# Causal attention beside a quantized FFN on eight cores: double-buffered weight rounding, and the second half of P·V moved to other PSUM banks

## The chip, the cores and the metric

The kernel runs on the 8 NeuronCores of one Trainium2 chip. All cores run the same program, each on its own rows, with no exchange between them. The metric is the device time of the slowest core in microseconds. Engines are named as in the profile: PE (TensorE), DVE (VectorE), ACT (ScalarE), POOL (GpSimd), SP (SyncE, which here only issues DMAs).

## What is computed

```python
xn = _layernorm(x, axis=-1)                       # x: (4, 4096, 2048) float32
K = xn @ Wk.T;  Q = xn @ Wq.T;  V = xn @ Wv.T     # all weights 2048 x 2048
probs = softmax(where(causal, Q @ K.T / sqrt(2048), -inf))
att = round(probs @ V * 10000) / 10000
xq = fake_quant(xn, 8, -1)        # scale per row
kq = fake_quant(kernel, 8, 0)     # scale per column of the FFN weight
bq = fake_quant(bias, 8, -1)
y = fake_quant(relu(xq @ kq + bq), 8, -1)
out = x + att + y
# fake_quant: s = max|x| / 127, round(x / s) clipped to +-127, times s
```

Two cores share a batch. Each makes K and V of the whole sequence and the output of every second block of 256 rows, 2048 rows in 16 tiles of 128.

## The kernel before, in words

`build_nc` writes the program as five stages with a barrier after each. Every instruction is recorded by `Prog.step` (a compute instruction) or `Prog.dma` with the `Buf` objects that it reads and writes. From these the waits are made: an instruction waits for the last writer of what it reads, and for the last writer and all readers since then of what it writes. This holds for instructions of its own engine too: PE then waits for sPE, the semaphore that its own earlier matmul raises when it is done. A `Buf` is a name and not a range of addresses, so one `Buf` for two PSUM banks makes a writer of the second wait for the writer of the first. Each engine issues in the order in which its steps were recorded, and so does each queue; nothing is reordered.

Stage 1 (L390 to L484): layernorm of all rows, V and K into HBM (`vS`, `kS`), PE L451 and L471. Stage 2 (to L640): layernorm and rounding of the core's own rows, Q into HBM (`qS`), PE L627.

Stage 3 quantizes the FFN weight, `fker`, 2048 x 2048, in 16 tiles of 128 rows (1 MB each). It has two passes over it, with two slots `fk` for the loads.

- The abs-max pass: SP loads a tile (L697), ACT takes the absolute value into `tab` (L699), DVE takes the running maximum over the tiles (L702 for the first, L704). There is one `tab`.
- A preamble: the maxima are transposed (L707), turned into reciprocals (L727), spread over all partitions (L737, L740), and the bias is quantized (L746 to L779).
- The rounding pass: POOL multiplies the tile by the reciprocal scales into `tab` (L786), ACT converts it into integers `ci3` (L788), DVE takes the remainder f3 from `tab` and `ci3` (L790), adds a correction (L793, reads f3 and `ci3`, writes r13) and scales (L796, writes the bf16 weight). There is one `tab`, one `ci3`, one `f3` and one `r13`. POOL's next multiply waits for L790, the last reader of `tab`.

Stage 4 is the FFN itself: 16 tiles, PE L845 with four PSUM banks a tile.

Stage 5 is attention, in 8 groups g of two query tiles (T = 0, 1). Group g looks at 512(g+1) keys:

- SP loads the Q tiles of the next group (`load_qt`, L943, 32 small DMAs), then x and the FFN result (L957, L959), then K in strips of 512 keys into two slots (`load_ktb`, L965, 16 DMAs a strip). The first strip of the next group is loaded ahead.
- QK: for each strip and each T, 16 matmuls into one bank of `psA` (L981); ACT or DVE copies the scores out (L991, L986), DVE takes the maximum (L995).
- First half of P·V: for each strip exp (L1021), transposes of P through the two banks `psTh` (L364), and 4 key chunks kc of 128. For each kc SP loads 128 x 1024 of V into one of two slots `vt` (L1030), and PE does 2 matmuls of 512 columns for each T (L1037). They sum up in `psB`, T = 0 in the first two banks, T = 1 in the other two, with one `Buf` each, bB[0] and bB[1].
- Second half of P·V, the other 1024 columns of V: nkc = 4(g+1) chunks, loads L1055, matmuls L1073. Here T = 0 sums up in `psA` (two banks, bA[0] and bA[1]) and T = 1 in `psN` (two banks, bT[0] and bT[1], the ones of the transposes).
- Behind each half, for each T, the evacuation: ACT L1093 reads the sums and writes the integers `ci4`, DVE L1096 reads the sums and `ci4`, L1099 reads `ci4` again, L1103 adds to the output tile. There is one `ci4`, so ACT's L1093 of T = 1 waits for DVE's L1099 of T = 0. PE's order is: first half, second half, QK of the next group.

A "step" is one kc of the second or first half: four matmuls, T = 0 twice, T = 1 twice. PSUM has 8 banks of 512 float32 columns: `psA` is 0 and 1, `psB` 2 to 5, `psN` and `psTh` 6 and 7.

## Time and profile before

| | us |
|---|---|
| median of 2 runs (5878.27 to 5885.0) | 5881.63 |
| the profiled execution's own time | 5880.86 |
| its span, on the slowest core (core 4) | 5879.3 |
| spans of the eight cores | 5795.6 to 5879.3 |
| PE busy | 3634.8 (62%) |
| DVE busy | 1085.1 (18%) |
| ACT busy | 678.6 (12%) |
| POOL busy | 208.2 (4%) |

The span runs from the first to the last instruction of one core; the time of an execution also has what lies around it, 1.6 us here. Busy time is that of an engine over the whole span, so it mixes the five stages. The granted clock is the share of TensorE's full speed that it was given: 1.00 is 2.4 GHz and 0.50 is 1.2 GHz. L12 is line 12 of the kernel before.

### The profile page before, as it was taken

What the parts mean: (1) busy time and instruction counts of PE and PEld (TensorE: products, weight loads), DVE (VectorE), ACT (ScalarE), POOL (GpSimd) and SP (SyncE); (2) the same over time, 40 slices, a digit from 0 to 9 for tenths busy, and PEclk for the clock granted to TensorE, in tenths of its full rate; (3) what the DMA queues carried; (4) which work ended last, traced back from release to release, by engine and by line L of the source; (5) the groups of instructions that cost most, each with busy time, mean ns of one, the idle gap of its engine ahead of it and who ended that gap; (6) DMA issues with size and microseconds to landing.
All of it is one profiled execution on the core that took longest, in us unless ns stands there. A gap on an engine that the chain in (4) does not pass through costs nothing.

```text
span 5879.3 us, 41336 instructions; the slowest of 8 cores (5795.6 to 5879.3 us)
## 1 busy us (share of the span) xinstructions
PE 3634.8 (62%) x9801; PEld 982.1 (17%) x9801; DVE 1085.1 (18%) x1473; ACT 678.6 (12%) x861; POOL 208.2 (4%) x87
## 2 busy tenths in 40 slices
PE   2787787787784375757821386144564747566776
PEld 0222222222221111111100022000111111111111
DVE  1110110010011403030037655011101011101001
ACT  1110110110101303021021121000000000000000
POOL 1000000000000000000003300010000000000000
PEclk9989999989987555555555598555555555555556
DMA  8110110110004101000032111132233232232422
GB/s 158 51 50 16 51 50 22 45 50 24 36 21 87 59 21 49 16 29 23 12 117 79 54 55 44 56 101 92 78 105 104 80 106 83 81 109 82 136 64 99
DMA packets 288082, 380.87 MB, mean 65 GB/s; under 512 B 123617, under 2 KB 222081, under 8 KB 273537
## 3 DMA queue, kind: packets, MB, share of 16 engines
q1 hardware_dynamic: 210866, 277.50, 14.8%
q10 hardware_dynamic: 69888, 75.51, 3.5%
q0 software_dynamic: 7120, 25.22, 2.6%
q8 instruction: 114, 1.87, 0.1%
q14 instruction: 94, 0.77, 0.0%
HBM read 327.83 MB, written 75.51 MB: 69 GB/s over the span
## 4 chain that ended last, share of the span: by engine, by line
PE 55%; DMA 15%; issue 14%; DVE 7%; ACT 4%; SPq 2%; POOL 2%; another core or an unknown queue 1%; DVEq 0%; ACTq 0%; POOLq 0%
PE pspool L471 13%; PE pspool L981 10%; DMA pool<-qS 8%; PE pspool L627 8%; PE pspool L451 8%; DMA pool<-vS 5%; PE pspool L845 5%; PE pspool L1037 4%; PE pspool L1073 2%; PE pspool L428 2%; POOL pool L786 2%; SPq L965 1%; PE pspool L364 1%; PE pspool L597 1%; PE pspool L581 1%
## 5 line engine op out<-in xcount | busy, mean ns | idle before, releaser
L981 PE MATMUL pspool<-pool 128*128 128x512 bf16 x1152 | 663.1, 586 | 652.3 <-DMA pool<-kS 475.4
L471 PE MATMUL pspool<-pool 128*128 128x512 bf16 x2048 | 751.9, 377 | 286.3 <-PE pspool L471 1.8
L627 PE MATMUL pspool<-pool 128*128 128x512 bf16 x1024 | 589.1, 587 | 272.2 <-ACT pool L631 128.7
L451 PE MATMUL pspool<-pool 128*128 128x512 bf16 x2048 | 492.7, 404 | 86.3 <-DMA pool<-wvT 41.3
L845 PE MATMUL pspool<-pool 128*128 128x512 bf16 x1024 | 276.7, 394 | 220.6 <-DMA pool<-nxS 182.4
L1037 PE MATMUL pspool<-pool 128*128 128x512 bf16 x576 | 299.9, 590 | 81.3 <-DMA pool<-vS 37.8
L471 PEld LDWEIGHTS pspool<-pool 128*128 128x128 bf16 x2048 | 196.0, 96 | 842.4 <-issue 837.9
L981 PEld LDWEIGHTS pspool<-pool 128*128 128x128 bf16 x1152 | 121.5, 105 | 1195.7 <-issue 1192.7
L1073 PE MATMUL pspool<-pool 128*128 128x512 bf16 x576 | 228.0, 544 | 113.6 <-DMA pool<-vS 111.5
L451 PEld LDWEIGHTS pspool<-pool 128*128 128x128 bf16 x2048 | 209.5, 102 | 366.1 <-issue 161.8
L627 PEld LDWEIGHTS pspool<-pool 128*128 128x128 bf16 x1024 | 107.2, 106 | 752.3 <-issue 751.0
L431 DVE COPY pool<-pspool 128x512 bf16<-128x512 bf16 x128 | 54.4, 425 | 954.1 <-PE pspool L428 954.1
L995 DVE TENSOR_REDUCE pool<-pool 128x1 f32<-128x512 f32 x72 | 49.4, 686 | 825.6 <-ACT pool L991 823.9
L475 ACT ACTIVATE pool<-pspool 128x512 bf16<-128x512 f32 x128 | 76.4, 597 | 991.0 <-PE pspool L471 938.2
L428 PE MATMUL pspool<-pool 128*128 128x128 bf16 x512 | 116.3, 259 | 119.9 <-DVE pool L351 62.5
L334 ACT ACTIVATE pool<-pool 128x2048 bf16<-128x2048 f32 x48 | 91.5, 1906 | 606.5 <-PE pspool L451 469.6
L1008 POOL TENSOR_TENSOR pool<-pool 128x2048 f32<-128x2048 f32 x16 | 78.4, 4919 | 2297.9 <-DVE pool L1005 2297.9
L845 PEld LDWEIGHTS pspool<-pool 128*128 128x128 bf16 x1024 | 83.5, 98 | 414.9 <-issue 355.1
L364 PE MATMUL pspool<-pool 128*128 128x128 bf16 x288 | 76.7, 266 | 116.2 <-ACT pool L1021 84.0
L991 ACT ACTIVATE pool<-pspool 128x512 f32<-128x512 f32 x56 | 33.4, 597 | 861.3 <-PE pspool L981 861.3
L581 PE MATMUL pspool<-pool 128*128 128x128 bf16 x256 | 61.9, 265 | 111.3 <-DVE pool L351 44.3
L584 DVE COPY pool<-pspool 128x512 bf16<-128x512 bf16 x64 | 27.2, 424 | 525.9 <-PE pspool L581 514.1
(118 smaller groups left out, 1951.5 us busy)
## 6 DMA issues: line engine op xcount, KB each, us to landing
pool<-kS SPq DMA_DIRECT2D x576, 128.0 KB, 3.0
pool<-vS SPq DMA_DIRECT2D x288, 256.0 KB, 2.7
pool<-emb SPq DMA_DIRECT2D x32, 1024.0 KB, 4.8
pool<-x_own SPq DMA_DIRECT2D x32, 1024.0 KB, 5.0
pool<-fker SPq DMA_DIRECT2D x32, 1024.0 KB, 5.0
vS<-pool ACTq DMA_DIRECT2D x32, 512.0 KB, 2.6
kS<-pool ACTq DMA_DIRECT2D x128, 128.0 KB, 1.9
out<-pool ACTq DMA_DIRECT2D x16, 1024.0 KB, 4.6
```

Of the source, the lines that this page charges most:

```text
L334: p.step("ACT", lambda e: e.activation(sq_ap, xap, AF.Copy, accum_out=s1), reads=[b_x], writes=[b_sq, btg])
L364: p.step("PE", lambda e, o=psl, i=sap: e.transpose(o, i, identb), reads=[b_src, b_identb], writes=[bT[half]])
L428: p.step("PE", lambda e, o=psl, i=sap: e.transpose(o, i, identb), reads=[b_xnb4[t], b_identb], writes=[bT[half]])
L451: e.matmul(pv, xnT[:, 512 * c + 128 * t:512 * c + 128 * t + 128], W2[:, E * c + fo:E * c + fo + fw], start=st, stop=sp),
L471: e.matmul(pk, W1[:, E * ce + 128 * ca:E * ce + 128 * ca + 128], xnT[:, 512 * ce:512 * ce + 512], start=st, stop=sp),
L581: p.step("PE", lambda e, o=psl, i=sap: e.transpose(o, i, identb), reads=[b_xnb24[t], b_identb], writes=[bT[half]])
L627: e.matmul(pk, WQ[:, E * ce + 128 * ca:E * ce + 128 * ca + 128], xnT2[:, 512 * ce:512 * ce + 512], start=st, stop=sp),
L786: p.step("POOL", lambda e, sl=sl: e.tensor_mul(tab, fk[sl], rcb), reads=[b_fk[sl], b_rcb], writes=[b_tab])
L845: st=(c == 0), sp=(c == NCH - 1): e.matmul(pv, nxt[sl][:, 128 * c:128 * c + 128], NK[:, E * c + fo:E * c + fo + fw], start=st, stop=sp),
L981: st=(c == 0), sp=(c == NCH - 1): e.matmul(pa, qt[par][T][:, 128 * c:128 * c + 128], ktb[ks][:, 512 * c:512 * (c + 1)], start=st, stop=sp),
L1037: st=(kc == 0), sp=(kc == nkc - 1): e.matmul(pv, PT[T][:, 128 * kc:128 * kc + 128], vt[vs_][:, fo:fo + fw], start=st, stop=sp),
L1073: st=(kc == 0), sp=(kc == nkc - 1): e.matmul(pv, PT[T][:, 128 * kc:128 * kc + 128], vt[vs_][:, fo:fo + fw], start=st, stop=sp),
```

## The change

In stage 3 `tab` and `ci3` get a second buffer each, `tabB` and `ci3B`, and tile c uses buffer c % 2, in both passes. `f3` and `r13` stay single (`fs3` and `b_fs3` list the same buffer twice).

In stage 5 the matmuls of the second half of P·V write `psB`, T = 0 its first two banks and T = 1 the other two, with bB[T] as their `Buf`; the evacuation reads both halves from there. `psA` is then written by QK only and the banks of `psN` by the transposes only.

```diff
+        o_tabB = al.take(E)
+        o_ci3B = al.take(E)
...
+        tabs = [tab, cf(o_tabB, E)]
+        cis = [ci3, cI(o_ci3B, E)]
+        fs3 = [f3, f3]
...
+        b_tabs = [b_tab, Buf("tabB")]
...
+        b_cis = [b_ci3, Buf("ci3B")]
+        b_fs3 = [b_f3, b_f3]
...
-            p.step("ACT", lambda e, sl=sl: e.activation(tab, fk[sl], AF.Abs),
-                   reads=[b_fk[sl]], writes=[b_tab])
+            p.step("ACT", lambda e, sl=sl: e.activation(tabs[sl], fk[sl], AF.Abs),
+                   reads=[b_fk[sl]], writes=[b_tabs[sl]])
...
-                p.step("DVE", lambda e: e.tensor_max(Mt, Mt, tab), reads=[b_tab, b_M], writes=[b_M])
+                p.step("DVE", lambda e, sl=sl: e.tensor_max(Mt, Mt, tabs[sl]),
+                       reads=[b_tabs[sl], b_M], writes=[b_M])
...
-            p.step("POOL", lambda e, sl=sl: e.tensor_mul(tab, fk[sl], rcb),
-                   reads=[b_fk[sl], b_rcb], writes=[b_tab])
-            p.step("ACT", lambda e: e.activation(ci3, tab, AF.Copy, bias=128.0),
-                   reads=[b_tab], writes=[b_ci3])
-            p.step("DVE", lambda e: e.scalar_tensor_tensor(
-                f3, tab, 128.0, ci3, op0=ALU.add, op1=ALU.subtract),
-                reads=[b_tab, b_ci3], writes=[b_f3])
+            p.step("POOL", lambda e, sl=sl: e.tensor_mul(tabs[sl], fk[sl], rcb),
+                   reads=[b_fk[sl], b_rcb], writes=[b_tabs[sl]])
+            p.step("ACT", lambda e, sl=sl: e.activation(cis[sl], tabs[sl], AF.Copy, bias=128.0),
+                   reads=[b_tabs[sl]], writes=[b_cis[sl]])
+            p.step("DVE", lambda e, sl=sl: e.scalar_tensor_tensor(
+                fs3[sl], tabs[sl], 128.0, cis[sl], op0=ALU.add, op1=ALU.subtract),
+                reads=[b_tabs[sl], b_cis[sl]], writes=[b_fs3[sl]])
...
-                                if T == 0 and PVW <= 512:
...
-                                elif T == 0:
-                                    pv = psA[:, fo:fo + fw]
-                                    wb_ = bA[fo // 512]
-                                else:
-                                    pv = psN[:, fo:fo + fw]
-                                    wb_ = bT[fo // 512]
+                                pv = psB[:, PVW * T + fo:PVW * T + fo + fw]
...
-                                    reads=[b_PT[T][kc // 4], b_vt[vs_]], writes=[wb_])
+                                    reads=[b_PT[T][kc // 4], b_vt[vs_]], writes=[bB[T]])
...
-                    if sweep == 0:
-                        pvh = psB[:, PVW * T:PVW * T + EH]
-                        rdb = [bB[T]]
...
+                    pvh = psB[:, PVW * T:PVW * T + EH]
+                    rdb = [bB[T]]
```

No instruction moves to another place; their waits change. PE before, in the first attention group, from the last step of the first half of P·V (L1037) to the second (L1073). z_vt0 and z_vt1 are the landings of V in its two slots, sPE, sAC and sDV the progress of PE, ACT and DVE:

```order
L1037 MATMUL pspool<-pool 128x512 [waits z_vt1]
L1037 MATMUL pspool<-pool 128x512 [waits sPE]
L1037 MATMUL pspool<-pool 128x512
L1037 MATMUL pspool<-pool 128x512 [waits sPE]
L1073 MATMUL pspool<-pool 128x512 [waits z_vt0]
L1073 MATMUL pspool<-pool 128x512 x3
L1073 MATMUL pspool<-pool 128x512 [waits z_vt1,sPE]
L1073 MATMUL pspool<-pool 128x512 [waits sPE] x3
```

The three matmuls behind the first of L1073 wait for nothing. The sPE of the later ones is for the matmul of the step before in the same bank. The same place in the changed kernel, where the lines are L1047 and L1072:

```order
L1047 MATMUL pspool<-pool 128x512 [waits z_vt1]
L1047 MATMUL pspool<-pool 128x512 [waits sPE]
L1047 MATMUL pspool<-pool 128x512
L1047 MATMUL pspool<-pool 128x512 [waits sPE]
L1072 MATMUL pspool<-pool 128x512 [waits z_vt0,sAC,sDV]
L1072 MATMUL pspool<-pool 128x512 [waits sPE]
L1072 MATMUL pspool<-pool 128x512 [waits sAC,sDV]
L1072 MATMUL pspool<-pool 128x512 [waits sPE]
L1072 MATMUL pspool<-pool 128x512 [waits z_vt1]
L1072 MATMUL pspool<-pool 128x512 [waits sPE]
L1072 MATMUL pspool<-pool 128x512
L1072 MATMUL pspool<-pool 128x512 [waits sPE]
```

The first matmul of each T now waits for ACT and DVE, and in each step the second and the fourth wait for the one ahead of them, as in L1047.

POOL before, at the start of the rounding pass (z_fk0 and z_fk1 are the landings of the weight tile, sPL POOL's own progress):

```order
L718 DMA pool<-rowS 1x16x128 [waits z_rowW]
L786 TENSOR_TENSOR pool<-pool 128x2048 [waits z_fk0,sDV,sAC]
L786 TENSOR_TENSOR pool<-pool 128x2048 [waits z_fk1,sPL,sAC,sDV]
L786 TENSOR_TENSOR pool<-pool 128x2048 [waits z_fk0,sPL,sAC,sDV]
L786 TENSOR_TENSOR pool<-pool 128x2048 [waits z_fk1,sPL,sAC,sDV]
```

And in the changed kernel, where the multiply is L796:

```order
L728 DMA pool<-rowS 1x16x128 [waits z_rowW]
L796 TENSOR_TENSOR pool<-pool 128x2048 [waits z_fk0,sDV,sAC]
L796 TENSOR_TENSOR pool<-pool 128x2048 [waits z_fk1,sAC]
L796 TENSOR_TENSOR pool<-pool 128x2048 [waits z_fk0,sPL,sAC,sDV]
L796 TENSOR_TENSOR pool<-pool 128x2048 [waits z_fk1,sPL,sAC,sDV]
```

The second multiply has lost its wait for DVE; from the third on each waits for the DVE instruction two tiles back.

## Rows read from the trace of the kernel before

**Rows 1.** Stages: length, busy us (x) of PE, PEld, DVE, ACT, POOL, PEclk, DMA, GB/s.

```profile
1850.00:2971.00 1121.00, 708.04 (x1536) 160.63 (x1536) 199.67 (x368) 209.88 (x257) 8.45 (x16) 0.50 0.14 38
2971.00:3321.00 350.00, 32.03 (x41) 8.96 (x41) 247.78 (x107) 65.21 (x35) 102.44 (x18) 0.50 0.29 99
3321.00:3640.00 319.00, 276.67 (x1024) 83.45 (x1024) 172.72 (x173) 61.72 (x45) 0.00 (x0) 0.94 0.17 48
3640.00:5880.00 2240.00, 1261.02 (x2592) 271.46 (x2592) 256.47 (x404) 130.01 (x236) 78.42 (x16) 0.53 0.28 91
```

**Rows 2.** Abs-max pass: timeline (start, length, what), L697's landing, one stretch.

```profile
2978.31 1.91 ACT L699 ACTIVATE pool<-pool 128x2048 f32<-128x2048 f32 x1 [7.82 <-DMA pool<-fker]
...
2986.10 1.91 ACT L699 ACTIVATE pool<-pool 128x2048 f32<-128x2048 f32 x1 [2.56 <-DVE pool L704]
...
2990.57 1.91 ACT L699 ACTIVATE pool<-pool 128x2048 f32<-128x2048 f32 x1 [2.56 <-DVE pool L704]
...
3046.25 2.29 DVE L704 TENSOR_TENSOR pool<-pool 128x2048 f32<-128x2048 f32 x1 [2.17 <-ACT pool L699]
...
DMA to landing us min/median/max: 4.7/4.8/7.9
...
2990.00:3000.00 10.00, 0.00 (x0) 0.00 (x0) 5.06 (x3) 4.31 (x3) 0.00 (x0) 0.50 0.72 255
```

**Rows 3.** The rounding pass: one row of the waits (us, times, longest), then the timeline.

```profile
POOL pool L786 <- DVE pool L790: 102.1, 15, 34.1
...
3103.38 4.49 POOL L786 TENSOR_TENSOR pool<-pool 128x2048 f32<-128x2048 f32 x1 [33.71 <-DVE pool L740]
...
3289.05 6.60 POOL L786 TENSOR_TENSOR pool<-pool 128x2048 f32<-128x2048 f32 x1 [4.71 <-DVE pool L790]
3291.41 6.39 DVE L796 SCALAR_TENSOR_TENSOR pool<-pool 128x2048 bf16<-128x2048 f32 x1
...
3300.36 6.61 POOL L786 TENSOR_TENSOR pool<-pool 128x2048 f32<-128x2048 f32 x1 [4.71 <-DVE pool L790]
...
3314.03 2.29 DVE L796 SCALAR_TENSOR_TENSOR pool<-pool 128x2048 bf16<-128x2048 f32 x1
```

**Rows 4.** Timeline of attention's first group, around the step between P·V's halves.

```profile
3828.24 0.58 PE L1037 MATMUL pspool<-pool 128*128 128x512 bf16 x1 [1.98 <-DMA pool<-vS]
3828.98 1.01 PE L1037 MATMUL pspool<-pool 128*128 128x512 bf16 x2
3830.14 2.17 PE L1037 MATMUL pspool<-pool 128*128 128x512 bf16 x4
...
3833.47 4.89 PE L1037 MATMUL pspool<-pool 128*128 128x512 bf16 x8 [0.43 <-DMA pool<-vS]
...
3838.88 1.86 PE L1073 MATMUL pspool<-pool 128*128 128x512 bf16 x4 [0.52 <-DMA pool<-vS]
...
3842.52 1.28 DVE L1096 SCALAR_TENSOR_TENSOR pool<-pspool,pool 128x1024 f32<-128x1024 f32 x1
3843.57 1.60 PE L1073 MATMUL pspool<-pool 128*128 128x512 bf16 x4 [0.31 <-DMA pool<-vS]
...
3846.36 1.02 PE L1073 MATMUL pspool<-pool 128*128 128x512 bf16 x4 [1.19 <-DMA pool<-vS]
```

**Rows 5.** Timeline of SP's queue and of PE at the turn of groups; waits.

```profile
3836.04 7.63 SPq L1055 DMA_DIRECT2D pool<-vS  x4
3843.76 65.69 SPq L943 DMA_DIRECT2D pool<-qS  x32
...
5786.47 70.50 SPq L1055 DMA_DIRECT2D pool<-vS  x32
...
3926.26 0.58 PE L981 MATMUL pspool<-pool 128*128 128x512 bf16 x1 [53.38 <-DMA pool<-kS]
...
PE pspool L981 <- DVE pool L1096: 15.5, 7, 2.5
```

**Rows 6.** Groups by line: L1037 and L1073 (busy us, mean ns | idle before).

```profile
L1037 PE MATMUL pspool<-pool 128*128 128x512 bf16 x576 | 299.9, 590 | 81.3 <-DMA pool<-vS 37.8
L1073 PE MATMUL pspool<-pool 128*128 128x512 bf16 x576 | 228.0, 544 | 113.6 <-DMA pool<-vS 111.5
```

More of the change, by code:

```diff
@@ L698, in build_nc @@
                 out=fk[sl], in_=fker[128 * c:128 * (c + 1), :]), writes=[b_fk[sl]])
-            p.step("ACT", lambda e, sl=sl: e.activation(tab, fk[sl], AF.Abs),
-                   reads=[b_fk[sl]], writes=[b_tab])
+            p.step("ACT", lambda e, sl=sl: e.activation(tabs[sl], fk[sl], AF.Abs),
+                   reads=[b_fk[sl]], writes=[b_tabs[sl]])
             if c == 0:
-                p.step("DVE", lambda e: e.tensor_copy(Mt, tab), reads=[b_tab], writes=[b_M])
-            else:
-                p.step("DVE", lambda e: e.tensor_max(Mt, Mt, tab), reads=[b_tab, b_M], writes=[b_M])
+                p.step("DVE", lambda e, sl=sl: e.tensor_copy(Mt, tabs[sl]),
+                       reads=[b_tabs[sl]], writes=[b_M])
+            else:
+                p.step("DVE", lambda e, sl=sl: e.tensor_max(Mt, Mt, tabs[sl]),
+                       reads=[b_tabs[sl], b_M], writes=[b_M])
         for t in range(NCH):
@@ L785, in build_nc @@
                 reads=[b_fk[sl]], writes=[b_fk[sl]])
-            p.step("POOL", lambda e, sl=sl: e.tensor_mul(tab, fk[sl], rcb),
-                   reads=[b_fk[sl], b_rcb], writes=[b_tab])
-            p.step("ACT", lambda e: e.activation(ci3, tab, AF.Copy, bias=128.0),
-                   reads=[b_tab], writes=[b_ci3])
-            p.step("DVE", lambda e: e.scalar_tensor_tensor(
-                f3, tab, 128.0, ci3, op0=ALU.add, op1=ALU.subtract),
-                reads=[b_tab, b_ci3], writes=[b_f3])
-            p.step("DVE", lambda e: e.scalar_tensor_tensor(
-                r13, f3, 0.5, ci3, op0=ALU.is_gt, op1=ALU.add),
-                reads=[b_f3, b_ci3], writes=[b_r13])
+            p.step("POOL", lambda e, sl=sl: e.tensor_mul(tabs[sl], fk[sl], rcb),
[5 more added lines that the diff above has]
+                reads=[b_tabs[sl], b_cis[sl]], writes=[b_fs3[sl]])
+            p.step("DVE", lambda e, sl=sl: e.scalar_tensor_tensor(
+                r13, fs3[sl], 0.5, cis[sl], op0=ALU.is_gt, op1=ALU.add),
+                reads=[b_fs3[sl], b_cis[sl]], writes=[b_r13])
             p.step("DVE", lambda e, c=c: e.scalar_tensor_tensor(
@@ L1059, in build_nc @@
                             for (fo, fw) in _splits(EH):
-                                if T == 0 and PVW <= 512:
-                                    pv = psA[:, fo:fo + fw]
-                                    wb_ = bA[0]
-                                elif T == 1 and PVW <= 512:
-                                    pv = psA[:, 512 + fo:512 + fo + fw]
-                                    wb_ = bA[1]
-                                elif T == 0:
-                                    pv = psA[:, fo:fo + fw]
-                                    wb_ = bA[fo // 512]
-                                else:
-                                    pv = psN[:, fo:fo + fw]
-                                    wb_ = bT[fo // 512]
+                                pv = psB[:, PVW * T + fo:PVW * T + fo + fw]
                                 p.step("PE", lambda e, pv=pv, T=T, kc=kc, vs_=vs_, fo=fo, fw=fw,
@@ L1080, in build_nc @@
                     rsc = tiny(sg, 2)
-                    if sweep == 0:
-                        pvh = psB[:, PVW * T:PVW * T + EH]
-                        rdb = [bB[T]]
-                    elif PVW <= 512:
-                        pvh = psA[:, 512 * T:512 * T + EH]
-                        rdb = [bA[T]]
-                    elif T == 0:
-                        pvh = psA[:, 0:EH]
-                        rdb = [bA[0], bA[1]]
-                    else:
-                        pvh = psN[:, 0:EH]
-                        rdb = [bT[0], bT[1]]
+                    pvh = psB[:, PVW * T:PVW * T + EH]
+                    rdb = [bB[T]]
                     p.step("ACT", lambda e, pvh=pvh, rsc=rsc: e.activation(
```

## The prediction

> **What bounds the kernel now.** I first read the busy times by stage [rows 1]. Barriers separate the stages, so each stage has its own limit and a gain in one passes whole into the start of the next. The change touches two of them: the quantization of the FFN weight (2971 to 3321 us) and attention (3640 to 5880 us). In the first the reader sees TensorE nearly empty, 32 us of 350, and VectorE busy for 248. In the second TensorE is busy for 1261 of 2240 us with a granted clock of 0.53, so it runs at its lower level, 1.2 GHz, for most of it.
>
> Then the timelines. The abs-max pass is a chain of two engines [rows 2]: an ACT Abs of 1.91 us, VectorE's max of 2.29, and an ACT that sat idle 2.56 us for VectorE because both share one buffer, `tab`. The pitch is 2990.57 − 2986.10 = 4.47 us. The rounding pass has a pitch of 3300.36 − 3289.05 = 11.31 us, and the table of waits says that GpSimd waits for L790 in it, 102.1 us in 15 times [rows 3]. In attention I read the step from the first half of P·V (L1037) to the second (L1073) [rows 4], the queue of SP [rows 5] and the means of the two matmul groups [rows 6].
>
> **Rounding pass: two buffers for `tab` and `ci3`.** Taken alone the wait of 102.1 us promises a pitch near the longer engine. The durations speak against it [rows 3]. The same GpSimd multiply takes 4.49 us where no wide VectorE instruction runs and 6.61 us where one does; L796 takes 6.39 us beside it and 2.29 us without. 2.29 + 4.1 = 6.4: the later one waits until the other is done and then runs at its own speed. So they run by turns, and a turn of the loop costs 4.49 + 3 × 2.29 = 11.36 us. The pitch is 11.31. The loop is already full, and another buffer adds no time in which both could run. What it does bring: the second multiply need not wait for L790 any more and runs at about 3108 us, in VectorE's preamble, where the first one [rows 3] ran at its full speed beside small copies out of PSUM. After that GpSimd is one tile ahead and the cadence is the same, until the last round has no multiply beside it. That takes one stay of 4.1 to 4.5 us out of the chain: **−4.3 us**. Bounds: 0 and −62 (the second is a rival below).
> The Trainium skill (SBUF — State Buffer, section Who interferes with whom) says the same of the cause: VectorE and GpSimd share one port pair, a VectorE instruction with two SBUF inputs contends with a GpSimd instruction that reads SBUF, and the loser blocks fully. The trace agrees, 6.39 against 2.29 us. By this rule the pass gains only the one multiply; with ports that don't interfere it would gain the 62 us.
>
> **Abs-max pass.** With two `tab` the ACT waits for a load instead. A load takes 4.8 us from issue to landing in the median, 4.7 to 7.9 [rows 2], and is issued when the Abs of its slot is done. Two slots give a pitch of (1.91 + 0.1 + 4.8 + 0.1)/2 = 3.5 us; VectorE alone would need 2.4. But the DMA engines are at 0.72 now, with 255 GB/s [rows 2]; at 4.47/3.5 times the rate that would be 0.92, so loads will stretch. I take 5.3 us for a load, pitch 3.7. From the first Abs to the end of the last max there are 3048.54 − 2978.31 = 70.2 us now; 14 rounds at 0.77 less give **−11 us**. Bounds: 0 (the DMA gives no more than now) and −20 (a pitch of 3.0, the 1.05 MB of a tile at 255/0.72 = 354 GB/s).
>
> **P·V, second half, in psB.** Three things change.
> 1. *A wait for the evacuation.* The first matmul of T=1 now needs L1096 of T=1 in the first half to be done, and that comes behind L1093, L1096 and L1099 of T=0, since `ci4` is single: it ends at 3842.52 + 1.28 = 3843.80 [rows 4]. TensorE issues in order, so all of the second half stands behind it. Before, this matmul pair began 0.86 us behind 3838.88, at 3839.74; now at 3843.87. That is 4.1 us, 4.4 at the end of this k step. The next step's load has long landed, so it follows at once, also 4.3 late. 8 groups × 4.3 = +34 us. Bounds per group: 3.3 and 4.6.
> 2. *A wait of each second matmul for its neighbour.* Before, four buffers stood for the four banks of L1073; now bB[T] stands for two banks, and the order of instructions shows a wait for sPE on each second matmul, as in L1037. The trace prices it. Four L1073 in a step take 1.86 us: starts 0.43 apart and 0.58 for the last. In L1037 the second starts 0.74 behind the first (3828.24 to 3828.98), the third 0.43 later, the fourth 0.73 after that [rows 4]. So a step takes 0.74 + 0.43 + 0.73 + 0.58 = 2.48 us. Now what sets the pitch: V has two slots, a slot is loaded again when its step is done, and some 3 us pass from there to the start of the step after the next (3838.88 + 1.86 = 3840.74 to 3843.57 is 2.83). Two steps take one step and one load, in L1037 5.23 and 5.41 us (starts at 3828.24, 3833.47, 3838.88). That is 2.66 a step. Now: the eight runs of V loads in the second half on SP, the first and the last of which stand in [rows 5], have 144 loads over 136 pitches and sum to 324.2 us: 2.38 a step. Past the first two steps of each group 144 − 16 = 128 steps remain, at 0.28 to 0.30 more: +37 us. Bounds: 0.16 and 0.40 a step, 20 and 51 us.
> 3. *psA and psN stay free.* The next group's first QK matmul no longer waits for L1096: 15.5 us in 7 times now. That counts only where nothing later is waited for. In the first six groups TensorE stops again after 32 matmuls, for K, for 53.38 us in the row [rows 5]. These K loads stand on SP behind 32 loads of Q, which take 65.69 us and start when the last V load is out. So there the gain is swallowed, and what delays the V loads passes whole. Only before the last group is no Q loaded, and there 15.5/7 = 2.2 us are won: **−2 us**.
> Together +34 + 37 − 2 = **+69 us** for attention.
>
> **Sum.** 5880.86 us is the profiled execution's own time, 1.6 above its span and within 1 us of the median of the runs. 5880.9 − 4.3 − 11 + 69 = 5934.6, so **5935 us**, 0.9% more.
>
> **The rivals.**
> *A, only the stall counts.* If the wait between banks were hidden, as the load sets the pitch, the steps would keep 2.38: 5880.9 − 15.3 + 8 × 3.5 − 2 = 5892. For it: L1073 waits for V 111.5 us in 117 times, so there is slack. Against: the slot is freed when the step is done, so a longer step pushes the load too, and L1037 shows 2.66 with the same waits.
> *B, the loop does overlap.* A pitch of 3 × 2.29 + 0.3 = 7.2 us instead of 11.31 takes 15 × 4.1 = 62 us off, 58 more than counted: 5877, not slower than before. For it: the wait table. Against: the durations. It decides if GpSimd can slip in without stretching L790 to L796.
> *C, the clock.* L1073 reaches 2.4 GHz in stretches, as in the four matmuls in 1.02 us at 3846.36 [rows 4]; mean 544 ns against 590 in L1037 [rows 6]. If the denser second half ran at 2.4 GHz throughout, a step would take 0.52 + 0.22 + 0.52 + 0.37 = 1.63 us (0.22 apart and 0.37 long in that row, and the 0.15 us of a wait that L1037 shows twice a step), the pitch (1.63 + 2.9)/2 = 2.27: −14 instead of +37, 5884 in all. Against: L1037, with the very waits, stays near 1.2.
> *D, slower by far.* The FFN stage that follows begins 15 us earlier. It ran at 0.94 of the clock [rows 1], while the Q projection just before the quantization stayed at 0.50 for 1121 us. If the clock does not rise, its 1024 matmuls take 0.43 us each, 437 us and not the 319 of the stage now: +118, 6053. It decides once TensorE stays at 1.2 GHz through the stage's first 50 us and beyond. Against: its matmuls have no waits between neighbours, and the start differs in nothing but its moment.
>
> **How the numbers follow.** Forecast 0.66 (its own range 5908 to 5962), A 0.13, B 0.06, C 0.07, D 0.03; 0.05 for mixtures beyond. The range of 5888 to 5966 takes in A and the forecast, most of the bounds of the terms. A measurement of this kernel tells about 2% from no change: 5764 to 5999. Faster by more than that needs B and C and more, 0.01; slower needs D or all terms at their upper ends, 0.05; within, 0.94.
>
> **What would show each step.** Right: Abs pitch near 3.7; loop pitch still 11.3 with 6.4 and 6.6 us pairs and an early second multiply; SP's runs of V loads in the second half 2.6 to 2.7 a load (the last group's 31 pitches over 82 us, not 70.50); the wait for K still near 53 us. Wrong: a loop pitch near 7, L1073's starts 0.43 apart for all four, a wait for V that vanishes, or a clock other than 0.5 to 0.55 in attention.

## The result, and the profile after

| | before | after |
|---|---|---|
| median, us (runs) | 5881.21 (14) | 5946.75 (15) |
| lowest, us | 5864.72 | 5938.50 |
| ratio, 95% interval | | 1.0094 [1.0068, 1.0120] |
| profiled execution: own time, slowest span | 5880.86, 5879.3 (core 4) | 6005.56, 6003.6 (core 2) |

The changed kernel is 0.9% slower. Ratios leave out executions in which a whole die was longer at a lower granted clock (up to 6355.99 us after the change). In the profiled execution of the changed kernel cores 2 and 3 reached stage 3 at 3030 and 3018 us, the other six at 2963 to 2972 like those of before, with nothing changed up to there, so its own time lies 59 us above the median. Therefore core 4 is compared in both, and lengths of stages are given as means over the eight cores.

| mean over 8 cores, us | before | after |
|---|---|---|
| stage 3, first Abs to first FFN matmul | 343.1 | 329.5 |
| from there to the first QK matmul | 461.3 | 468.0 |
| attention, first QK matmul to the end | 2061.5 | 2145.0 |
| of it SP's eight runs of V loads, second half | 319.5 | 404.0 |

Stage 3 gave 13.6 us and attention took 83.5, which is what the second half of P·V took: its runs of V loads are 84.5 us longer.

The stages on core 4 (columns as in [rows 1]):

```profile
1850.00:2966.00 1116.00, 708.22 (x1536) 159.83 (x1536) 199.72 (x368) 209.71 (x256) 5.12 (x10) 0.50 0.14 38
2966.00:3298.00 332.00, 32.01 (x41) 8.97 (x41) 242.42 (x107) 65.11 (x35) 100.28 (x18) 0.50 0.30 104
3298.00:3607.00 309.00, 269.29 (x1024) 83.08 (x1024) 170.29 (x171) 61.72 (x45) 0.00 (x0) 0.97 0.17 49
3607.00:5928.00 2321.00, 1337.99 (x2592) 253.44 (x2592) 258.93 (x406) 130.09 (x236) 78.13 (x16) 0.51 0.27 88
```

Against [rows 1] PE is busy for 77 us more in attention with the same 2592 matmuls, and its granted clock went from 0.53 to 0.51. FFN kept its high clock. The abs-max pass on core 4, the same view as [rows 2] (Abs is L707, max L713):

```profile
2972.19 1.91 ACT L707 ACTIVATE pool<-pool 128x2048 f32<-128x2048 f32 x1 [7.61 <-DMA pool<-fker]
...
2998.28 1.91 ACT L707 ACTIVATE pool<-pool 128x2048 f32<-128x2048 f32 x1 [1.97 <-DMA pool<-fker]
3001.98 1.91 ACT L707 ACTIVATE pool<-pool 128x2048 f32<-128x2048 f32 x1 [1.78 <-DMA pool<-fker]
...
3030.40 2.29 DVE L713 TENSOR_TENSOR pool<-pool 128x2048 f32<-128x2048 f32 x1 [1.87 <-ACT pool L707]
```

One stretch of the same pass (columns as in the stages):

```profile
2990.00:3000.00 10.00, 0.00 (x0) 0.00 (x0) 5.99 (x3) 5.54 (x3) 0.00 (x0) 0.50 0.79 271
```

From issue to landing a load (L705) now takes:

```profile
DMA to landing us min/median/max: 4.7/5.3/7.8
```

The Abs now waits for its load and no longer for VectorE. The pass takes 3032.69 − 2972.19 = 60.5 us and not 70.2. The load takes 5.3 us in the median, as the prediction had put in, and not 4.8. The DMA share rose from 0.72 to 0.79 only, and not to the 0.92 that the prediction gave as the reason. The rounding pass, as [rows 3] (multiply L796, f3 L800, scaling L806), first the wait, then the timeline:

```profile
POOL pool L796 <- DVE pool L800: 90.5, 14, 29.6
```

```profile
3087.50 8.96 POOL L796 TENSOR_TENSOR pool<-pool 128x2048 f32<-128x2048 f32 x2 [33.71 <-DVE pool L750]
...
3259.54 6.60 POOL L796 TENSOR_TENSOR pool<-pool 128x2048 f32<-128x2048 f32 x1 [4.50 <-DVE pool L800]
3261.90 6.40 DVE L806 SCALAR_TENSOR_TENSOR pool<-pool 128x2048 bf16<-128x2048 f32 x1
...
3270.64 6.60 POOL L796 TENSOR_TENSOR pool<-pool 128x2048 f32<-128x2048 f32 x1 [4.50 <-DVE pool L800]
...
3291.09 2.29 DVE L806 SCALAR_TENSOR_TENSOR pool<-pool 128x2048 bf16<-128x2048 f32 x1
```

The first two multiplies run in one stretch of 8.96 us, 4.48 each; after that the pairs of 6.60 and 6.40 us return. The pitch is 3270.64 − 3259.54 = 11.10 us.

The step between the halves of P·V in the first group, as [rows 4] (L1072 is the second half, L1085 the evacuation's DVE instruction):

```profile
3808.59 1.32 PE L1072 MATMUL pspool<-pool 128*128 128x512 bf16 x2 [1.64 <-DVE pool L1085]
3811.10 1.28 DVE L1085 SCALAR_TENSOR_TENSOR pool<-pspool,pool 128x1024 f32<-128x1024 f32 x1
3812.53 3.64 PE L1072 MATMUL pspool<-pool 128*128 128x512 bf16 x6 [2.62 <-DVE pool L1085]
3816.98 2.48 PE L1072 MATMUL pspool<-pool 128*128 128x512 bf16 x4 [0.81 <-DMA pool<-vS]
3819.89 2.48 PE L1072 MATMUL pspool<-pool 128*128 128x512 bf16 x4 [0.43 <-DMA pool<-vS]
```

T=0's pair waits 1.64 us for the evacuation of T=0. T=1's pair waits until L1085 of T=1 is done at 3811.10 + 1.28 = 3812.38 and starts at 3812.53. A step is then 2.48 us long, not 1.86. Later steps of the last group, in the same view:

```profile
5882.31 4.80 PE L1072 MATMUL pspool<-pool 128*128 128x512 bf16 x8 [0.47 <-DMA pool<-vS]
5887.58 5.04 PE L1072 MATMUL pspool<-pool 128*128 128x512 bf16 x8 [0.48 <-DMA pool<-vS]
```

Each row is two steps, 5.27 us from start to start: 2.64 a step, at 1.2 GHz. The queue of SP and the first K wait of the timeline, then the table of waits of PE, on core 4, as [rows 5]:

```profile
3816.67 68.57 SPq L953 DMA_DIRECT2D pool<-qS  x32
...
5818.55 88.23 SPq L1065 DMA_DIRECT2D pool<-vS  x32
...
3902.03 2.79 PE L991 MATMUL pspool<-pool 128*128 128x512 bf16 x4 [56.81 <-DMA pool<-kS]
```

```profile
PE pspool L991 <- DMA pool<-kS: 486.0, 7, 155.1
PE pspool L1072 <- DMA pool<-vS: 48.0, 71, 3.1
PE pspool L1072 <- DVE pool L1085: 34.4, 16, 2.6
```

The last run of V loads takes 88.23 us and not 70.50. QK (L991) has no wait for L1085 any more, but its wait for K in the first group became longer, 56.81 us against 53.38. The groups, as [rows 6]:

```profile
L1072 PE MATMUL pspool<-pool 128*128 128x512 bf16 x576 | 308.6, 598 | 126.1 <-DMA pool<-vS 48.0 <-DVE pool L1085 34.4
L1047 PE MATMUL pspool<-pool 128*128 128x512 bf16 x576 | 296.9, 586 | 79.4 <-DMA pool<-vS 36.2
```

The second half's matmuls, 544 ns before, take 598 ns and are now those of the first half.

### The profile page after: what moved, and what is told of

Read it like the earlier page. It is cut to its first block, busy times and chain, and to the rows that moved or that the text cites. A ratio compares the mean times of both kernels' runs of the same rounds, so it can differ in the third digit from the quotient of the medians.

```text
span 6003.6 us, 41045 instructions; the slowest of 8 cores (5864.0 to 6003.6 us)
## 1 busy us (share of the span) xinstructions
PE 3749.7 (62%) x9801; PEld 965.2 (16%) x9801; DVE 1079.5 (18%) x1473; ACT 678.6 (11%) x861; POOL 205.8 (3%) x87
## 3 DMA queue, kind: packets, MB, share of 16 engines
q1 hardware_dynamic: 210866, 277.50, 14.4%
## 4 chain that ended last, share of the span: by engine, by line
PE 55%; DMA 16%; issue 16%; DVE 7%; ACT 3%; SPq 2%; another core or an unknown queue 1%; DVEq 0%; ACTq 0%; POOLq 0%
PE pspool L471 14%; PE pspool L991 9%; DMA pool<-qS 8%; PE pspool L627 8%; PE pspool L451 8%; DMA pool<-vS 5%; PE pspool L855 4%; PE pspool L1047 4%; PE pspool L1072 3%; PE pspool L428 2%; SPq L975 1%; PE pspool L364 1%; PE pspool L597 1%; PE pspool L581 1%; DMA pool<-fker 1%
## 5 line engine op out<-in xcount | busy, mean ns | idle before, releaser
L991 PE MATMUL pspool<-pool 128*128 128x512 bf16 x1152 | 650.6, 575 | 661.8 <-DMA pool<-kS 500.5
L471 PE MATMUL pspool<-pool 128*128 128x512 bf16 x2048 | 800.3, 400 | 286.1
L627 PE MATMUL pspool<-pool 128*128 128x512 bf16 x1024 | 589.2, 587 | 272.1 <-ACT pool L631 128.7
L451 PE MATMUL pspool<-pool 128*128 128x512 bf16 x2048 | 494.2, 404 | 85.0 <-DMA pool<-wvT 40.4
L855 PE MATMUL pspool<-pool 128*128 128x512 bf16 x1024 | 276.7, 393 | 213.4 <-DMA pool<-nxS 175.3
L1072 PE MATMUL pspool<-pool 128*128 128x512 bf16 x576 | 304.1, 590 | 127.4 <-DMA pool<-vS 47.8
L1047 PE MATMUL pspool<-pool 128*128 128x512 bf16 x576 | 301.6, 595 | 81.4 <-DMA pool<-vS 38.3
L991 PEld LDWEIGHTS pspool<-pool 128*128 128x128 bf16 x1152 | 120.3, 104 | 1190.3 <-issue 1186.1
L431 DVE COPY pool<-pspool 128x512 bf16<-128x512 bf16 x128 | 54.3, 425 | 1003.0 <-PE pspool L428 1003.0
L428 PE MATMUL pspool<-pool 128*128 128x128 bf16 x512 | 116.8, 260 | 123.0 <-DVE pool L351 65.7
L855 PEld LDWEIGHTS pspool<-pool 128*128 128x128 bf16 x1024 | 83.5, 98 | 407.7 <-issue 348.3
L581 PE MATMUL pspool<-pool 128*128 128x128 bf16 x256 | 61.9, 266 | 111.7 <-DVE pool L351 44.7
L1031 ACT ACTIVATE pool<-pool 128x512 bf16<-128x512 f32 x72 | 51.5, 716 | 628.5 <-PE pspool L364 376.8
```

Source lines behind the costliest of these rows:

```text
L428: p.step("PE", lambda e, o=psl, i=sap: e.transpose(o, i, identb), reads=[b_xnb4[t], b_identb], writes=[bT[half]])
L451: e.matmul(pv, xnT[:, 512 * c + 128 * t:512 * c + 128 * t + 128], W2[:, E * c + fo:E * c + fo + fw], start=st, stop=sp),
L471: e.matmul(pk, W1[:, E * ce + 128 * ca:E * ce + 128 * ca + 128], xnT[:, 512 * ce:512 * ce + 512], start=st, stop=sp),
L581: p.step("PE", lambda e, o=psl, i=sap: e.transpose(o, i, identb), reads=[b_xnb24[t], b_identb], writes=[bT[half]])
L627: e.matmul(pk, WQ[:, E * ce + 128 * ca:E * ce + 128 * ca + 128], xnT2[:, 512 * ce:512 * ce + 512], start=st, stop=sp),
L855: st=(c == 0), sp=(c == NCH - 1): e.matmul(pv, nxt[sl][:, 128 * c:128 * c + 128], NK[:, E * c + fo:E * c + fo + fw], start=st, stop=sp),
```

## Experiments

Twelve kernels. Where a kernel's total and its stages disagree, both are given. "V2" is the sum of SP's eight runs of V loads in the second half, a mean over eight cores; 319.5 us before, 404.0 after.

### Is it the second half of P·V, or stage 3?

The first kernel has the stage 3 of the change and the attention of before, the second the other way round.

```diff
 # e1_stage3_only, against the changed kernel: attention as before:
-                                    reads=[b_PT[T][kc // 4], b_vt[vs_]], writes=[bB[T]])
+                                    reads=[b_PT[T][kc // 4], b_vt[vs_]], writes=[wb_])
 # e2_pv_only: stage 3 as before; attention as in the change
```

> Only the two buffers for tab and ci3 of the weight quantization; P.V as before. My theory (GpSimd and VectorE take turns, so the loop stays full): loop pitch 11.1 to 11.3 us, abs-max pitch 3.7, and the kernel 15 to 17 us faster than before, give or take 8 us for the moment at which the clock rises in the FFN stage. Rival (the buffers let the two engines overlap): loop pitch near 7, 60 us more off. Rival (the abs-max pass is bound by the DMA already): 5 us off in all.

Measured: stage 3 takes 328.7 us (before 343.1), attention 2063.4 (2061.5), ratio 1.0024 [0.9991, 1.0057]. The 14.4 us are there in all eight cores' stage 3, but the ratio shows none of them. The part from the first FFN matmul to attention took 476.0 us in the mean here, 461.3 before; the cores spread from 457 to 497. On core 4 the stretches of it are (same columns as the stages):

```profile
3310.00:3320.00 10.00, 8.05 (x28) 1.67 (x26) 0.00 (x0) 0.00 (x0) 0.00 (x0) 1.00 0.00 0
3320.00:3400.00 80.00, 71.30 (x245) 21.22 (x244) 40.98 (x44) 16.46 (x12) 0.00 (x0) 0.84 0.17 47
3400.00:3500.00 100.00, 87.98 (x289) 24.23 (x288) 50.59 (x49) 16.46 (x12) 0.00 (x0) 0.82 0.16 48
3500.00:3600.00 100.00, 88.77 (x343) 28.85 (x342) 62.83 (x66) 20.84 (x17) 0.00 (x0) 0.96 0.21 59
```

The clock had reached 1.00 and then fell to 0.82 to 0.84 for some 180 us. That is not tied to the earlier start: on cores 4 to 7 of the changed kernel the same part takes 462.4 us, and in the kernel with P·V alone, whose stage 3 is untouched, cores 6 and 7 show 475 and 483. The single runs show the gain where this clock does not cover it: the four quickest of the ten lie between 5861.6 and 5868.5 us, in the middle 10.9 below the 5876.21 of before, and the other six between 5902 and 6034. So some 11 of the 14 us reach the total in four runs of ten. These four were picked by their times after the fact, so this is a hint and no proof; a price of the earlier start was not found.

> Only the move of the second half of P.V into psB; the weight quantization as before. Theory (stall of 4.1 us a group and a longer step): 65 to 85 us slower than before, attention stage alone. Rival (only the stall counts): 25 to 30 us slower. Together with the run of the other part the two must add up to the changed kernel, +50 to +65.

Measured: attention 2146.4 us, V2 403.9, stage 3 343.1; ratio 1.0200 [1.0151, 1.0250]. The stage says +84.9, as in the full change (+83.5). The lowest of its four runs, 5961.8 us, is 85.6 above the 5876.21 of before, which is what the stages say; the others lie higher, and so does the ratio. In the profiled one (6014.59 us) the slowest core reached stage 3 at 3022 us, 50 us later than most others, with the same code up to there; why was not tried.

### The wait for the neighbour and the wait for the evacuation, apart

Both are put on the kernel before, each without the other. The names `nb` give T's two banks one more `Buf` in common and nothing else.

```diff
 # e4_neighbour_wait
+        b_nb = [Buf("nb0"), Buf("nb1")]
...
-                                    reads=[b_PT[T][kc // 4], b_vt[vs_]], writes=[wb_])
+                                    reads=[b_PT[T][kc // 4], b_vt[vs_]], writes=[wb_, b_nb[T]])
 # e5_stall_only
-                                    reads=[b_PT[T][kc // 4], b_vt[vs_]], writes=[wb_])
+                                    reads=[b_PT[T][kc // 4], b_vt[vs_]],
+                                    writes=[wb_, bB[T]] if kc == 0 and fo == 0 else [wb_])
```

> The kernel before, with one extra Buf for each T in the second half of P.V, so that each second matmul waits for the one ahead as in the first half; banks and evacuation as before, no stall at its start. Theory (a longer step frees its V slot later, so it lengthens the pitch by half of its own growth): step 2.48 us, pitch 2.66 to 2.8 against 2.38, 37 to 55 us slower than before. Rival (the load sets the pitch and hides it): under 10 us. Rival (it is a matter of the clock alone): the starts stay 0.43 apart but the mean rises from 544 to 590 ns, 10 to 20 us.

> The kernel before, with the first matmul of each T in the second half of P.V also waiting for the readers of psB, though it writes psA and psN. The stall of the change without the neighbour waits. Theory: the first step of each second half ends 3.8 to 4.4 us later, 8 times, 28 to 36 us slower in all. Rival (the stall is taken back, since V is loaded meanwhile and the following steps catch up, or come in a denser row that lifts the clock): under 15 us.

Measured: with the neighbour wait alone attention takes 2117.3 us, **+55.8**, V2 373.2, ratio 1.0096 [1.0080, 1.0112]. With the stall alone 2090.0 us, **+28.5**, V2 349.7, ratio 1.0080 [1.0021, 1.0138]. That ratio would be 47 us; one run of 5963.76 us is in it, and the medians differ by 25.7. By the stages 55.8 + 28.5 = 84.3, and both together took 84.9: the two terms add, and nothing else in P·V counts. Timeline of PE with the neighbour wait, core 4:

```profile
5053.07 0.58 PE L1074 MATMUL pspool<-pool 128*128 128x512 bf16 x1 [0.47 <-DMA pool<-vS]
5053.80 1.01 PE L1074 MATMUL pspool<-pool 128*128 128x512 bf16 x2 [0.15 <-PE pspool L1074]
...
5058.41 0.59 PE L1074 MATMUL pspool<-pool 128*128 128x512 bf16 x1 [0.44 <-DMA pool<-vS]
...
5063.65 0.58 PE L1074 MATMUL pspool<-pool 128*128 128x512 bf16 x1 [0.34 <-DMA pool<-vS]
```

The second matmul starts 0.73 behind the first; two steps take 5.34 and 5.24 us. The group of the second half of P·V in this kernel, core 4, as [rows 6]:

```profile
L1074 PE MATMUL pspool<-pool 128*128 128x512 bf16 x576 | 303.9, 592 | 94.8 <-DMA pool<-vS 51.0
```

Against [rows 6] PE is busy 76 us longer here and waits 60 us less for V; in the mean of the eight cores it is 82.4 longer (220.9 to 303.3) and 65.7 less (111.7 to 46.0). So most of a longer step is taken out of the wait for V, and the rest is paid. With the stall alone, first the timeline, then the group:

```profile
4995.74 1.01 PE L1073 MATMUL pspool<-pool 128*128 128x512 bf16 x2 [1.65 <-DVE pool L1097]
4999.67 2.72 PE L1073 MATMUL pspool<-pool 128*128 128x512 bf16 x6 [2.92 <-DVE pool L1097]
5003.56 3.57 PE L1073 MATMUL pspool<-pool 128*128 128x512 bf16 x8 [1.17 <-DMA pool<-vS]
5008.40 3.57 PE L1073 MATMUL pspool<-pool 128*128 128x512 bf16 x8 [1.27 <-DMA pool<-vS]
5013.16 1.02 PE L1073 MATMUL pspool<-pool 128*128 128x512 bf16 x4 [1.18 <-DMA pool<-vS]
```

```profile
L1073 PE MATMUL pspool<-pool 128*128 128x512 bf16 x576 | 225.4, 537 | 137.0 <-DMA pool<-vS 98.1 <-DVE pool L1097 36.9 <-PE pspool L1073 1.7
```

After the same stall TensorE gets to 2.4 GHz within seven steps (1.02 us for four matmuls). With the neighbour wait its mean stays at 592 ns.

### The neighbour wait taken away

Each half's two banks get a `Buf` each, in the first half on the kernel before and in both halves on the changed one.

```diff
+        bBk = [[Buf("psB00"), Buf("psB01")], [Buf("psB10"), Buf("psB11")]]
...
-                                reads=[b_PT[T][kc // 4], b_vt[vs_]], writes=[bB[T]])
+                                reads=[b_PT[T][kc // 4], b_vt[vs_]], writes=[bBk[T][fo // 512]])
...
-                        rdb = [bB[T]]
+                        rdb = bBk[T]
```

> The kernel before with one Buf for each bank of psB in the first half of P.V, so that its second and fourth matmul of a step no longer wait for their neighbour; the second half untouched. Theory (the neighbour wait costs 0.3 us twice a step also there): starts 0.43 apart, a step of 1.86 us, a strip's four steps about 8.4 us and not 10.1, 36 strips, 40 to 65 us faster; the eight runs of V loads of the second half unchanged near 320 us. Rival (exp and transposes or the V loads bound the first half): under 15 us.

> The changed kernel with one Buf for each bank of psB in both halves of P.V; the stall at the start of the second half stays. Theory: the second half gets back the 54 us that the run with the neighbour wait alone cost, the first half gains as in the run beside it (40 to 65), so 95 to 120 us faster than the changed kernel, 35 to 60 faster than before; V loads of the second half 350 us, as with the stall alone. Rival (psB itself, its banks or their turn-round, slows the matmuls): the second half keeps its 400 us.

Measured: on before 0.9827 [0.9763, 0.9892], attention 1989.7 us (−71.8). On the changed kernel 0.9873 [0.9793, 0.9954] against before, attention 2012.6 us, 132.4 less than with the change as it is. One half is worth 71.8, the other 132.4 − 71.8 = 60.6, against the 55.8 of putting it in. The expectations had 40 to 65 and 95 to 120; in attention both gains came out larger. What is left of the change's cost in attention is 2012.6 − 1989.7 = 22.9 us, where the stall alone cost 28.5. So the new banks as such cost no more than the stall; the larger part came from naming two banks with one `Buf`. One thing moved that nobody expected: QK's matmuls took 551 ns in the mean of the cores and not 586, and the waits for K were 50 us longer (507.6 against 458.0 without the change), so that this brought about nothing. Why QK ran faster was not tried.

### Is it the V loads through which the delay passes?

Four slots for V instead of two.

```diff
-        o_vt = [al.take(EH // 2), al.take(EH // 2)]
+        o_vt = [al.take(EH // 2) for _ in range(4)]
...
-                        vs_ = kc % 2
+                        vs_ = kc % 4
```

> The changed kernel with four slots for V and not two; the waits between neighbours and the stall stay. Theory (the pitch is (step + load) / 2 with two slots): with four the load is hidden and the pitch falls to the step alone, 2.32 us; second half from 404 to about 345 us, V waits of both halves gone, 70 to 95 us faster than the changed kernel. Rival (the DMA queue's rate sets the pitch): under 15 us.

> The kernel before with four slots for V. Theory (pitch (step + load) / 2, hidden with four; denser matmuls and the clock rises to 2.4 GHz as it did in the run on the changed kernel): the second half runs at 0.22 to 0.43 a matmul until the V loads' own rate binds, near 1.3 to 1.7 us a step; attention 150 to 200 us shorter than before. Rival (what made the run on the changed kernel so quick was psB and psA's freedom, TensorE never stopping at the turn of a group): attention less than 110 us shorter.

Measured: on the changed kernel attention 1954.8 us (−190.2), median 5864.08; on before 1859.3 (−202.2), median 5773.51. No ratio could be given for either, their runs spread from 5756.32 to 6194.39 and from 5663.72 to 5895.93, so only the stages are used (in the profiled execution of the second, four cores reached stage 3 at 3089 to 3209 us, which is outside the stage compared). The gain on the changed kernel is twice the expected 70 to 95, since the expectation left out that denser steps also raise the clock. The group of the second half on core 4, first with the change, then without:

```profile
L1072 PE MATMUL pspool<-pool 128*128 128x512 bf16 x576 | 232.2, 488 | 79.8 <-DVE pool L1085 35.2 <-DMA pool<-vS 1.5 <-PE pspool L1072 1.4
```

```profile
L1073 PE MATMUL pspool<-pool 128*128 128x512 bf16 x576 | 146.3, 400 | 28.0 <-DMA pool<-vS 26.3 <-PE pspool L1073 0.6
```

The wait for V fell from 48.0 to 1.5 us on the changed kernel, so with two slots it is the load that follows each step. With four the change costs 1954.8 − 1859.3 = 95.5 us, more than with two (83.5). In the second half of P·V alone it costs 130 us (means over the cores: busy 146.5 to 225.5, idle 29.4 to 80.8): with hardly a wait for V left, little of the longer step is taken out of it. QK, again faster (551 against 584 ns), gives some 33 back. The mean of a matmul fell to 400 ns without it and to 488 with it; denser steps bring the higher clock, and the neighbour wait takes part of it away.

### The rounding pass: GpSimd's share

On the changed kernel the multiply moves from GpSimd to VectorE, with the load, the multiply and the conversion recorded one tile ahead.

```diff
-        for c in range(NCH):
+        def q_front(c):
...
-            p.step("POOL", lambda e, sl=sl: e.tensor_mul(tabs[sl], fk[sl], rcb),
+            p.step("DVE", lambda e, sl=sl: e.tensor_mul(tabs[sl], fk[sl], rcb),
...
+        q_front(0)
+        for c in range(NCH):
+            sl = c % 2
+            if c + 1 < NCH:
+                q_front(c + 1)
```

> The changed kernel with the multiply of the rounding pass on VectorE, one tile ahead, and GpSimd out of the loop. Theory (the two engines take turns, so a multiply of 4.49 us on GpSimd costs the chain more than one of 2.29 on VectorE): loop pitch 4 x 2.39 = 9.6 us against 11.1, no L806 over 2.3 us, the weight quantization 15 to 20 us shorter. Rival (GpSimd works beside VectorE and takes load off it): pitch longer than 11.1.

Measured: stage 3 305.9 us, 23.6 less than the change; ratio to before 1.0065 [1.0022, 1.0108]. Core 5, timeline:

```profile
3208.80 2.29 DVE L796 TENSOR_TENSOR pool<-pool 128x2048 f32<-128x2048 f32 x1
3211.00 2.29 DVE L806 SCALAR_TENSOR_TENSOR pool<-pool 128x2048 f32<-128x2048 f32 x1
...
3213.39 2.29 DVE L809 SCALAR_TENSOR_TENSOR pool<-pool 128x2048 f32<-128x2048 f32 x1
3215.78 2.29 DVE L812 SCALAR_TENSOR_TENSOR pool<-pool 128x2048 bf16<-128x2048 f32 x1
3217.99 2.29 DVE L796 TENSOR_TENSOR pool<-pool 128x2048 f32<-128x2048 f32 x1
```

None of these is stretched any more, and the pitch is 3217.99 − 3208.80 = 9.19 us, four times 2.29. VectorE alone does all the work faster than it does three quarters of it beside GpSimd (11.10). That is what taking turns on SBUF predicts: GpSimd's 4.49 us cost VectorE 4.1, its own multiply costs 2.29. The order of one tile ahead is part of this kernel too; the two were not tried apart. The Trainium skill (SBUF — State Buffer, Who interferes with whom) states that the two engines share one exclusive port pair; 6.40 against 2.29 us for the same instruction agrees.

### Does freeing psA and psN bring anything without the Q loads in the way?

The Q tiles' `Buf`s are made with `slices=True`, so that a tile's 16 loads don't wait for one another.

```diff
-        b_qt = [[Buf("qt00"), Buf("qt01")], [Buf("qt10"), Buf("qt11")]]
+        b_qt = [[Buf("qt00", slices=True), Buf("qt01", slices=True)],
+                [Buf("qt10", slices=True), Buf("qt11", slices=True)]]
```

> The kernel before; the Q loads of one tile no longer wait for each other on SP (the Buf of a Q tile is marked as written in slices). Theory (what TensorE waits for at the turn of a group is K, and K stands on SP behind 32 Q loads that wait for each other's landing, 2.05 us each): a Q load costs SP its issue alone, 0.3 to 0.6 us, the 65 us become 10 to 20, the wait for K at the turn falls from 53 us to under 10, six times, and the wait of 155 us at the start of the stage to 60 to 110: 300 to 380 us faster. Rival (the small rows of Q make the DMA itself slow): SP's stretch shrinks but the wait for K stays over 40 us, under 60 us faster.

> The same edit on the changed kernel. Theory: the wait for K no longer swallows what psA's freedom gives at the turn of a group (2.2 us, 7 times) beside the 13 us of the quantization, so it stands 50 to 62 us behind the run on the kernel before, in the attention stage alone 70 and not 85 us behind. Rival (the turn of the group was worth nothing at all): attention 85 us behind.

Measured: on before 0.9441 [0.9374, 0.9507], on the changed kernel 0.9522 [0.9505, 0.9539]. Attention takes 1801.2 and 1886.8 us: the change costs 85.6, as it did with the Q loads in the way (83.5). That is the rival's number; the expected 70 did not come. The wait for K on core 4, of before, then of the changed kernel with this edit:

```profile
PE pspool L982 <- DMA pool<-kS: 110.1, 7, 70.0
```

```profile
PE pspool L992 <- DMA pool<-kS: 118.7, 7, 70.3
```

Before lost 16.2 us more to L1097 at the turn of the groups, which the changed kernel doesn't; it waits 8.6 us longer for K on this core, and 21.9 in the mean of the eight (111.6 to 133.5). TensorE still stops for K, so a QK that starts earlier ends no earlier. The edit itself is the largest single gain of the study: 32 loads of Q took 65.69 us on SP [rows 5] and 17.80 in this kernel's timeline.

### All together

Before, with the change's stage 3, the multiply on VectorE, a `Buf` per bank in the first half, four V slots and free Q loads. The second half stays in psA and psN.

```diff
+        bBk = [[Buf("psB00"), Buf("psB01")], [Buf("psB10"), Buf("psB11")]]
+        o_vt = [al.take(EH // 2) for _ in range(4)]
+        b_qt = [[Buf("qt00", slices=True), Buf("qt01", slices=True)],
...
+            p.step("DVE", lambda e, sl=sl: e.tensor_mul(tabs[sl], fk[sl], rcb),
```

> The kernel before with the two buffers of the quantization, its multiply on VectorE, one Buf for each bank in the first half of P.V, four slots for V, and Q loads that don't wait for each other; the second half stays in psA and psN. Sum of the parts: -37 for the quantization, -76 for the banks, -150 for the V slots (partly the same time), -300 or more for the Q loads: 5300 to 5450 us, clearly faster than both kernels. Against a plain sum: with the waits gone the K loads of 18 us a strip bind QK if the clock rises.

Measured: 5203.41 us, ratio 0.8795 [0.8752, 0.8839], faster than both kernels and below the expected 5300. Stage 3 takes 306.3 us, attention 1469.0 (−592.5), more than the three gains in attention by themselves (71.8 + 202.2 + 260.3 = 534.3). The expectation's 18 us for a strip of K is the time of two: [rows 5] has 32 loads in 17.86 us, and a strip has 16. The second half's matmuls on core 4:

```profile
L1091 PE MATMUL pspool<-pool 128*128 128x512 bf16 x576 | 137.4, 378 | 49.4 <-DMA pool<-vS 47.4 <-PE pspool L1091 1.4
```

The mean is 378 ns against 544 [rows 6], and most of the idle time left in this group is still a wait for V.

## Why the prediction was right, and where its terms were off

The forecast was 5935 us, in the range of 5888 to 5966; measured 5946.75, and "within 2%" held. By its own steps:

- **Rounding pass, −4.3.** Right in kind: the second multiply was early, the pairs of 6.6 and 6.4 us stayed, the loop was already full. Rival B fell: a pitch of 11.10 and not 7.2. What was missed is 11.31 − 11.10 = 0.21 us a tile, some 3 us: GpSimd's wait before each multiply went from 4.71 to 4.50 us. Why by that much was not tried.
- **Abs-max pass, −11.** Measured 70.2 − 60.5 = −9.7, with a pitch of 3.77 (45.2 us in 12 rounds) and the load as the thing waited for. Together stage 3 lost 13.6 us in the mean (16.8 on core 4; the 7.1 outside this pass are about the 4.3 and 3 above), forecast 15.3.
- **Wait for the evacuation, +34.** The moment was right: T=1's pair starts 0.15 us behind the end of L1085 [rows 4 and the same view after]. The price was 28.5 us, 3.6 a group and not 4.3. That the delay passes whole was too much: in the kernel with the stall alone TensorE waits 37.0 us for the evacuation in the mean of the cores, and attention grows by 28.5. The difference is in the waits for V: V is loaded during the stall, and the second half waits 104.0 us for it and not 111.7. The clock has no part in it, a matmul takes 531 ns in the mean against 530.
- **Wait for the neighbour, +37.** The mechanism was right and the size too small: +55.8. The term that was mis-sized is "at 0.28 to 0.30 more". Its 2.66 a step came from two pairs in the first group. Over all groups the V loads with this wait sum to 373.2 us in 136 pitches, 2.74 each; before, over the eight cores, 319.5/136 = 2.35, where core 4 alone gave 2.38. The difference is 0.39 a step, and it counts in 136 pitches and not in 128: 53 us. It grows with the group: the run of 4 loads took 0.6 us more, that of 32 13.8 us (70.50 to 84.28 in the mean of the cores), 0.44 a pitch. In the large groups of before many steps ran at 2.4 GHz, which [rows 4] shows for one step of the first. In the last group on core 4 twelve of 32 steps take 1.02 us, this one among them:

```profile
5817.39 1.02 PE L1073 MATMUL pspool<-pool 128*128 128x512 bf16 x4 [0.60 <-DMA pool<-vS]
```

  With the neighbour wait the second half ran at 592 ns in the mean and not at 530. So a step (busy time and idle time other than for V, mean of the cores) grew from 1.55 to 2.42 us, by 0.88 and not by the 2.48 − 1.86 = 0.62 of the first group. By the rule that the prediction used in its rival C, a pitch of (step + load)/2, half of it is paid: 0.44, near the 0.39. The upper bound of the prediction, 0.40 a step or 51 us, came near.
- **psA and psN free, −2.** Right as far as can be seen. The wait for L1096 (15.5 us) went and the waits for K rose by 10.6, from 475.4 to 486.0 us on core 4 (12.5 in the mean of the cores), which leaves 3 to 5 us; of these the sum of the single kernels, 84.3 against 83.5 and 84.9, shows nothing beyond 1 us. Letting the Q loads run freely did not bring the rest out (85.6 against 83.5), so it is K itself and not only the Q loads ahead of it that swallows the gain.
- **Sum.** 28.5 + 55.8 − 13.6 = +70.7 us by stages, forecast +54. The interval of the ratio is +40 to +71 us; the medians differ by 65.5. Luck had a part in it: the stall was 5 us too dear and the neighbour wait 19 too cheap, and the two errors partly cancel. The mechanisms were the forecast ones, the size of the larger term was not.
- **The rivals.** A (the stall alone counts) is out: V2 grew by 53.7 us with the neighbour wait alone. C (the second half at 2.4 GHz) went the other way, 598 ns instead of 544. D (FFN stays at 1.2 GHz) did not happen: 0.97 of the clock.

## What to carry to other kernels

A `Buf` that covers two banks is a wait between neighbouring matmuls, 0.3 us each at 1.2 GHz, and it can keep the clock low. Waiting for the loads afterwards does not hide it if a load can only start when that very step has freed its slot: with two slots 0.39 of 0.88 us a step were paid here. Look for the wait on the engine's own semaphore in the order of instructions before judging a change of banks. Where GpSimd and VectorE each have wide elementwise work on SBUF like this one, add up their undisturbed durations, don't take the larger. And price a pitch over a whole run of loads of each kind, since its mean also has the stretches at the other clock level in it.

## What the runs showed of the hardware

- The granted clock can hold a value between its two levels for a long stretch. In FFN of the changed kernel cores 0 and 1 ran at 0.81 while cores 2 and 3 of the same die had 1.00. Core 0 and core 3, the same 120 us (columns as in the stages):

```profile
3460.00:3580.00 120.00, 104.50 (x340) 29.01 (x345) 63.99 (x62) 20.58 (x15) 0.00 (x0) 0.81 0.18 53
...
3460.00:3580.00 120.00, 104.96 (x413) 33.36 (x412) 74.70 (x73) 25.44 (x19) 0.00 (x0) 1.00 0.20 58
```

  In the kernel with stage 3 alone it was cores 2 and 3 and cores 4 and 5; in the profile of before no core shows it. Cores 0 and 1 took 488 and 486 us for the part between stage 3 and attention, the others 450 to 470. The Trainium skill (TensorE: Matmul & The Clock Gate, Seeing it yourself) tells of a third state of 0.81 that takes a whole die; here it took two cores of a die and left the other two.
- On core 4 the mean matmul of the second half took 598, 544, 488, 400 and 378 ns as waits in and between the steps were taken away. A gain in waiting brought a gain in clock: four slots for V gave 202 us on before, more than the 37.8 + 111.5 = 149.3 us for which both halves wait for V there [rows 6]. In the mean of the cores 108 us of it are waits for V, and 94 are busy time of the same matmuls.
- In attention the eight cores fall into two sets of four: about 2041 us (cores 0, 2, 5, 6) and 2082 before, 2118 (the odd ones) and 2172 after. All have the same amount of work; of each pair 0/1, 2/3, 4/5, 6/7 one core is in each set, and which one differs between executions. The difference lies in the waits for K: 436 to 445 us in the one set and 475 to 479 in the other before, 445 to 452 and 486 to 501 after. With free Q loads the two sets are gone on the changed kernel (1871 to 1895 us). Why was not tried.
